# New hand-written orders for all five engines of an adaLN, attention and FFN kernel

## The reference, cut to what matters

```python
x = x + attn(moe(x, cond))       # 8 experts of width 64, top 2, and a shared one; banded linear attention; layer norm
x = x + ffn(attn2(x, mask, cond))  # 16 heads of 64, l2-normed q and k, position bias, softmax, layer norm
# attn2:
xn = ln(x, g_norm); q = xn @ Wq; k, v = split(xn @ Wkv)
sim = l2norm(q) * q_scale @ (l2norm(k) * k_scale).T * 8 + bias + causal mask
out = ln((softmax(sim) @ v) @ Wout, g_out)
# ffn: 128 -> 512 -> 512 -> 512 -> 128
h = silu(z @ w1 * s1) * (z @ w2 * s2)
h = gelu(h @ h1 * s); h = gelu(h @ h2 * s); return h @ w3 * s3
```

## Time and profile before

| | |
|---|---|
| three timed runs | 715.15, 715.75, 716.42 us, median 715.75 |
| profiled execution | 719.08 us, of which 717.1 us is the span from first to last instruction |
| mean granted TensorE clock | 0.983 of full |
| busy | TensorE 679.9, VectorE 547.5, ScalarE 528.1, GpSimd 359.6 us |
| fill, first pass | 0 to about 76.8, 76.8 to 136 us |
| a steady pass | 80.2 us |

### The profile page before, as it was taken

The page is one execution under the profiler, slowest core; times in us unless marked ns, Lnnn a source line. Parts: engine busy times, 40 slices in busy tenths (PEclk is TensorE's granted clock), DMA queues, the critical chain, the costliest instruction groups (busy, mean ns, idle before and its releaser), DMA issues.

```text
span 717.1 us, 20509 instructions
## 1 busy us (share of the span) xinstructions
PE 679.9 (95%) x7232; PEld 537.5 (75%) x7232; DVE 547.5 (76%) x1719; ACT 528.1 (74%) x1629; POOL 359.6 (50%) x410
## 2 busy tenths in 40 slices
...
GB/s 284 9 111 90 123 2 16 82 22 1 2 87 60 1 2 12 134 3 1 3 104 43 1 3 24 122 2 1 2 118 30 1 1 25 16 17 1 17 8 8
DMA packets 33587, 28.50 MB, mean 40 GB/s; under 512 B 4288, under 2 KB 29008, under 8 KB 33104
## 3 DMA queue, kind: packets, MB, share of 16 engines
...
...
## 4 chain that ended last, share of the span: by engine, by line
PE 57%; DVE 14%; ACT 9%; issue 7%; POOL 4%; DVEq 0%; ACTq 0%; POOLq 0%
PE ps_M L1314 30%; PE ps_z L1466 8%; DVE sb_sm L1187 5%; PE ps_S L1453 5%; PE ps_S L1438 4%; PE ps_M L1367 4%; PE ps_M L1498 3%; ACT sb_sm L830 3%; PE ps_S L1422 2%; PE ps_M L1397 2%; ACT sb_hT L795 2%; POOL sb_rq L697 1%; DVE sb_nmx L1194 1%; DVE sb_hAl L1024 1%; POOL sb_biasm L707 1%
## 5 line engine op out<-in xcount | busy, mean ns | idle before, releaser
L830 ACT ACTIVATE sb_sm<-sb_sm,sb_nmx 128x65 f32<-128x65 f32 (+3 forms) x512 | 178.1, 352 | 14.4 <-DVE sb_nmx L1194 14.1
L715 POOL TENSOR_TENSOR sb_sm<-sb_sm,sb_rden 128x128 f32<-128x128 f32 (+3 forms) x128 | 93.2, 738 | 126.4 <-DVE sb_rden L1198 126.1
L707 POOL TENSOR_TENSOR sb_biasm<-sb_bias,sb_maskn 128x128 f32<-128x128 f32 (+3 forms) x128 | 113.0, 894 | 49.6 <-DVE sb_maskn L1159 26.5
L1187 DVE SCALAR_TENSOR_TENSOR sb_sm<-ps_S,sb_rq,sb_biasm 128x65 f32<-128x65 f32 (+3 forms) x512 | 112.2, 292 | 24.0 <-PE ps_S L1438 19.5
L697 POOL TENSOR_TENSOR sb_rq<-sb_qss,sb_mhalf 128x16 f32<-128x16 f32 x32 | 93.6, 2949 | 28.8 <-DVE sb_qss L1169 28.8
L830 ACT ACTIVATION_READ_ACCUMULATOR sb_sm<-sb_sm,sb_nmx 128x1 f32 x512 | 97.1, 190 | 0.0
L1466 PE MATMUL ps_z<-sb_wout,sb_oT 128*128 128x128 f32 x512 | 69.1, 282 | 0.0
L1466 PEld LDWEIGHTS ps_z<-sb_wout,sb_oT 128*128 128x128 f32 x512 | 64.4, 193 | 4.3 <-ACT sb_oT L842 0.8
L842 ACT ACTIVATE sb_oT<-ps_S,sb_cols 128x256 f32<-128x256 f32 x128 | 52.9, 467 | 16.5 <-PE ps_S L1453 13.1
L1194 DVE TENSOR_REDUCE sb_nmx<-sb_sm 128x4 f32<-128x132 f32 (+3 forms) x128 | 59.3, 475 | 0.3
L767 ACT ACTIVATE sb_gs<-ps_M 128x512 f32<-128x512 f32 x39 | 23.2, 596 | 46.2 <-PE ps_M L1314 46.1
...
## 6 DMA issues: line engine op xcount, KB each, us to landing
...
sb_vrep<-values SPq DMA_DIRECT2D x16, 256.0 KB
sb_xg<-in_xT SPq DMA_DIRECT2D x8, 256.0 KB, 3.4
sb_xs<-in_x SPq DMA_DIRECT2D x8, 256.0 KB, 6.8
...
sb_hA<-in_h SPq DMA_DIRECT2D x2, 1024.0 KB, 7.2
out_y<-sb_res SPq DMA_DIRECT2D x7, 256.0 KB, 7.0
values<-sb_vs SPq DMA_DIRECT2D x16, 64.0 KB
```

Source lines behind the costliest of these rows:

```text
L707: pool.tensor_tensor(masked_bias(j % 4)[:, :, 1:wide], relative(bias0, i), maskn[:, j // 4, 0:wide - 1].unsqueeze(1).broadcast_to([128, 4, ...
L715: pool.tensor_tensor(p, p, stat(rden, g, j).unsqueeze(2).broadcast_to([128, 4, wide - 1]), ALU.mult)\
L830: ins = act.activation(p[:, t], p[:, t], ACT.Exp, bias=least[:, t:t + 1], accum_out=total[:, t:t + 1])
L1187: ins = dve.scalar_tensor_tensor(scored(g, j)[:, t], bank(g, "sim", n, odd)[:, first:first + wide], rq[:, col:col + 1], masked_bias(j % 4) ...
```

## The change

Of the 30 lists, 24 are written anew: all but the drain lists of TensorE, VectorE and GpSimd and the last three of SyncE. Each list holds exactly the items that it held before, in another order. Nothing else in the file is changed. [...] The lists that the prediction speaks of:

```diff
     "pe fill": """
-        lg.0 warm.0-2 pb.0-1 warm.3-6 rw.0 lg.1-2 exp.0-1 lg.3-4 exp.2 pb.2 lg.5-7 pb.3 exp.3-4 down.0 qkv.0
-        scores.0 mix.0 warm.7 fl.0-1 warm.8-10 fl.2 warm.11-13 xnT.0 warm.14 wr.0 warm.15-16 q.0 kv.0 q.1-4
-        qs.0-3 q.5-7 kT.0 warm.17 qs.4-7 warm.18-21
+        lg.0 pb.0 warm.0-4 rw.0 pb.1 lg.1-2 exp.0-1 lg.3 exp.2 lg.4 pb.2 lg.5 exp.3 lg.6-7 exp.4 pb.3 down.0
+        warm.5 qkv.0 scores.0 mix.0 warm.6 fl.0 warm.7-9 fl.1 warm.10-11 wr.0 warm.12-13 xnT.0 warm.14 fl.2
+        warm.15 kv.0 q.0-5 qs.0-3 q.6-7 warm.16 kT.0 warm.17 qs.4-7 warm.18-21
     "pe steady": """
-        sim.0 exp.0-3 sim.1 exp.4 down.0 zT.0 sim.2-3 qkv.0 l1.0 sim.4 l1.1 sim.5 l1.2-3 scores.0 l2.0-3 mix.0
-        PV.0 l3.0-2 sim.6-7 xnT.0 l3.3 kv.0 z.0 q.0 z.1 PV.1 l4.0 PV.2 q.1-2 z.2 q.3-4 qs.0-3 q.5-7 z.3 qs.4-7
-        kT.0 z.4 PV.3 z.5-7
+        sim.0 exp.0-1 sim.1 exp.2-4 down.0 zT.0 sim.2-3 qkv.0 l1.0 sim.4 l1.1 sim.5 l1.2-3 scores.0 l2.0-3 mix.0
+        PV.0 l3.0 sim.6-7 l3.1-2 xnT.0 l3.3 kv.0 q.0 z.0 PV.1 q.1 z.1 q.2 l4.0 z.2 PV.2 q.3-4 qs.0-3 q.5-7 z.3
+        qs.4-7 z.4 kT.0 PV.3 z.5-7
     "pe seventh": """
-        sim.0-1 exp.0 sim.2 exp.1-4 down.0 sim.3 zT.0 sim.4 qkv.0 scores.0 l1.0 sim.5 l1.1-3 mix.0 PV.0 l2.0
+        sim.0 exp.0-2 sim.1 exp.3 sim.2 exp.4 down.0 zT.0 sim.3 qkv.0 sim.4 l1.0 scores.0 l1.1-2 sim.5 l1.3
...
     "pe last": """
-        sim.0-2 l3p.2-3 sim.3-4 zT.0 l4p.0 l1.0 PV.0 l1.1 z.0 l1.2-3 z.1 l2.0 sim.5-6 l2.1-2 PV.1 l2.3 z.2 sim.7
+        sim.0-3 l3p.2-3 sim.4 zT.0 l4p.0 l1.0 PV.0 l1.1 z.0 l1.2-3 z.1 l2.0 sim.5-6 l2.1-2 PV.1 l2.3 z.2 l3.0
...
     "act start": """
-        xh.0 ph.4 rw.0 exp.0-2 ex.0 exp.3 ex.1 exp.4 ex.2-3 down.0 ex.4 qkv.0 ex.5-6 ph.5 ex.7 PV.0 ex.8 PV.1
+        xh.0 ph.4 rw.0 exp.0-2 ex.0 exp.3 ph.5 ex.1 exp.4 ex.2-3 down.0 qkv.0 ex.4-7 PV.0 ex.8 PV.1 ex.9 ln2.0
...
     "dve fill": """
-        cg.0 pb.0 rt.0 x0.0 pb.1 rt.1-4 rw.0 pl.0 wl.0 pb.2 exp.0 pb.3 exp.1 nk.0 exp.2 rt.5 exp.3 pl.1 rt.6
-        exp.4 rt.7 down.0 xl.0 rt.8 maskn.0 qkv.0 scores.0 mix.0 pl.2 ln1.0 rt.9 xnT.0 pl.3 nk.1 q.0 kv.0 q.1-4
-        vs.0 q.5-7 ssq.0 ssc.0
+        cg.0 pb.0 rt.0 pb.1 rt.1-4 rw.0 wl.0 x0.0 pl.0 exp.0 pb.2 exp.1 pb.3 xl.0 pl.1 nk.0 exp.2-3 rt.5 exp.4
+        rt.6-7 down.0 rt.8 qkv.0 scores.0 mix.0 ln1.0 rt.9 pl.2-3 xnT.0 kv.0 q.0-3 maskn.0 nk.1 q.4-7 vs.0 ssq.0
+        ssc.0
     "dve start": """
-        rw.0 xl.0 pl.4 exp.0 sim.0 exp.1 max.0 exp.2 inv.0 max.1 exp.3 sim.1 inv.1 max.2 exp.4 max.3 sim.2 tp.0
+        rw.0 xl.0 pl.4 exp.0 sim.0 exp.1 max.0 exp.2 inv.0 max.1 exp.3 sim.1 inv.1 max.2 exp.4 max.3 sim.2
...
     "pool start": """
-        bias.4-5 pn.0 bias.6 pn.1 xb.0 bias.7-8 pn.2-4 bias.9 pn.5-6 bias.10 ln1.0 pn.7 bias.11-12 ln2.0
+        bias.4-5 pn.0-1 bias.6-7 pn.2 bias.8-9 pn.3 bias.10 pn.4 bias.11 ln1.0 bias.12 xb.0 bias.13 pn.5-6 ln2.0
...
     "sp fill": """
-        hw.0 lx.0 ls.0 vst.0 wr.0 lm.0 vb.0-1
+        lx.0 ls.0 hw.0 vst.0 vb.0 wr.0 lm.0 vb.1
     "sp start": """
-        hw.1 lx.0 ls.0 wb.0 vst.0 vb.0 lm.0 vb.1
+        lx.0 hw.1 wb.0 vst.0 vb.0 lm.0 ls.0 vb.1
     "sp steady": """
-        vst.0 lx.0 wb.0 vb.0 ls.0 l4.0 vb.1 lm.0
+        vst.0 vb.0 wb.0 ls.0 l4.0 lm.0 lx.0 vb.1
```

More of the change, by code:

```diff
@@ L64 @@
+        warm.15 kv.0 q.0-5 qs.0-3 q.6-7 warm.16 kT.0 warm.17 qs.4-7 warm.18-21
     """,
     "pe start": """
-        rw.0 exp.0 sim.0-1 exp.1-3 sim.2 exp.4 down.0 sim.3-4 qkv.0 scores.0 mix.0 PV.0 sim.5-6 z.0 xnT.0 PV.1
-        q.0 z.1 sim.7 z.2 kv.0 q.1 PV.2 z.3 q.2-3 z.4 PV.3 q.4 qs.0-3 q.5-7 z.5 qs.4-7 kT.0 z.6-7
+        rw.0 exp.0 sim.0-1 exp.1-3 sim.2 exp.4 down.0 sim.3 qkv.0 scores.0 mix.0 sim.4 PV.0 sim.5-6 z.0 xnT.0
+        z.1 PV.1 q.0 sim.7 z.2 kv.0 PV.2 q.1 z.3 q.2 z.4 q.3 z.5 PV.3 q.4 qs.0-3 q.5-7 qs.4-7 kT.0 z.6-7
@@ L86 @@
     "act fill": """
-        wh.0 xh.0 rx.0 ph.0 pb.0-1 rw.0 exp.0 pb.2 exp.1 pb.3 exp.2 ph.1 exp.3 rx.1 pb.4 exp.4 ph.2 down.0 qkv.0
-        fl.0 ph.3 ln2.0 fl.1-2 xnT.0 wr.0 q.0-3 kd.0 q.4-7 kT.0
+        xh.0 rx.0 pb.0 wh.0 pb.1 ph.0 rw.0 exp.0-2 ph.1 pb.2 exp.3 pb.3 ph.2 exp.4 rx.1 pb.4 down.0 qkv.0 fl.0
+        ph.3 ln2.0 fl.1 wr.0 xnT.0 fl.2 q.0-3 kd.0 q.4-7 kT.0
     """,
     "act start": """
-        xh.0 ph.4 rw.0 exp.0-2 ex.0 exp.3 ex.1 exp.4 ex.2-3 down.0 ex.4 qkv.0 ex.5-6 ph.5 ex.7 PV.0 ex.8 PV.1
@@ L102 @@
-        q.5-7 ex.12-15 PV.4-5 l3.0 kd.0 l3.1 PV.6-7 kT.0
+        xh.0 exp.0-1 ex.0 exp.2 ex.1 exp.3-4 ex.2-3 down.0 zT.0 ex.4-5 qkv.0 ex.6 l1.0 h1.0 l1.1-2 h1.1-2 l1.3
+        ex.7 h1.3 PV.0-1 ex.8-10 l2.0 ln2.0 h2.0 xnT.0 l2.1-2 h2.1 PV.2 h2.2 q.0-1 PV.3 q.2-3 l2.3 ex.11 q.4-6
+        h2.3 q.7 ex.12-15 PV.4-5 kd.0 l3.0-1 PV.6-7 kT.0
     """,
     "act last": """
-        ex.0-3 l3p.2-3 ex.4 zT.0 ex.5-6 l1.0 PV.0 l1.1 h1.0-1 l1.2 PV.1 l1.3 h1.2-3 ex.7-10 l2.0 h2.0 PV.2 l2.1
-        h2.1 PV.3 l2.2-3 h2.2-3 ex.11-13 l3.0-3 zTd.0 ex.14-15 l1d.0 PV.4 l1d.1 h1d.0 PV.5 h1d.1 l1d.2 h1d.2
@@ L123 @@
+        tp.0-1 inv.2-3 down.0 sim.3 max.4 tp.2 max.5 tp.3 qkv.0 inv.4 scores.0 max.6 tp.4 inv.5 max.7 mix.0
+        sim.4 inv.6-7 max.8 ln1.0 tp.5 max.9 sim.5 inv.8 tp.6-7 max.10 sim.6 max.11 inv.9 maskn.0 xnT.0 tp.8
+        max.12 inv.10 tp.9 inv.11 tp.10 max.13 tp.11 sim.7 inv.12 max.14 q.0 inv.13 max.15 kv.0 tp.12 inv.14
+        tp.13 inv.15 tp.14-15 q.1-2 pl.5 q.3-7 ssq.0 ssc.0 vs.0
     """,
     "dve steady": """
-        xl.0 ln3.0 sim.0 exp.0-1 max.0-1 exp.2-3 sim.1 exp.4 max.2 zT.0 max.3 inv.0-2 down.0 zl.0 sim.2 max.4
@@ L126 @@
[L126 to L129, removed]
+        xl.0 ln3.0 sim.0 exp.0 max.0 exp.1 max.1 exp.2-3 sim.1 exp.4 max.2 zT.0 max.3 inv.0-1 down.0 zl.0 sim.2
```

68 lines of the change are left out of this document (35 added, 33 removed).

## The result

| | us |
|---|---|
| before, on the same chip | median 716.09 (715.15 to 718.72, 4 runs) |
| after | median 725.45 (723.06 to 730.28, 4 runs) |
| ratio | 1.0133, 95% interval 1.0073 to 1.0193 |
| predicted | 719.6, range 712.5 to 727 |

The sign and the place are those of the forecast, the size is not: +9.4 us measured, +3.9 forecast.

The account below looks back on a forecast made before the run. TensorE, busy 95% of its 717.1 us span, was taken as the bound. Fill and first pass +4.0, steady +1.0, seventh -1.8, last pass +0.7 sum to +3.9: median 715.75 becomes 719.6, range 712.5 to 727.

Parts of the forecast that it names:

- First pass, the term that decides: First pass: early ph.5 makes ScalarE wait 4.4 us for h2, exp.4 +3.7; fill and first pass together +4.0.
- the prediction's own sign: First pass, profile after: ScalarE idle 3 to 5 us at about 84 to 89, ended by the DMA into sb_hA.
- The clock behind the wait: First pass: qkv's matmuls at the low clock after longer idle time, only in the upper bound of +6.5.
- Fill, -1.8: Fill: low-clock stretch gone (1.4), first expert about 1.0 earlier, wr ahead of xnT 0.6 late; bounds -3.5 and +1.0.
- The row of "lg" items: Fill: three "lg" items in a row from 28.74, then low clock 31.0 to 34.4; spreading them might save 1.4 us.
- Its difference is laid on 715.75: Whole kernel: the sum is made against the profiled 719.08 us and its difference applied to the timed median.
- Steady, +1.0: Five steady passes: TensorE's new order costs +0.2 a pass; lx moved later costs nothing.
- Rival 2: Steady passes: lx lands late, exp.0 up to 2.2 us late in each of five; 724.6, at worst 730; chance 0.14.
- Seventh, -1.8: Seventh pass: 0.7 wait and small ones removed, a second VectorE wait covered, shorter switches; bounds -2.5 and +1.0.
- The 0.7 wait: Seventh pass: TensorE's longest wait, for VectorE, removed by exp.0-1 standing ahead of sim.1.
- Last pass, +0.7: Last pass: sim.3 waits for VectorE +1.0, 0.5 back at l4p, zT in the drain +0.2; bounds -0.5 and +1.5.
- Rival 1: First pass: h2 lands in time, its load taking 4.8 instead of 9.5 us; 713 to 714.9, say 713.7; chance 0.27.

Follow-up runs that it names:

- e1: After, with only ScalarE's copy of raw h2 (ph.5) moved back to its old place between ex.6 and ex.7; 717.9 us, ratio 1.0014.
- e4: After, with the load of h2 issued straight behind the store of the values, ahead of both spreads, ph.5 still early; 716.4 us, ratio 0.9987.
- e2: Before, with only ScalarE's copy of raw h2 (ph.5) moved to its new place right behind exp.3; 719.92 us, ratio 1.0047.
- r1: After, with only vs.0 moved back in VectorE's fill list, from behind q.7 to behind q.3; 720.73 us, ratio 1.0051.
- r2: After, with the load of h2 issued behind the first of the two spreads, ahead of wr, lm, the second spread and lx; 720.63 us, ratio 1.0047.
- g1: After, with h2 loaded early as in e4, SyncE's old steady list (lx second) and last-pass sim.3 behind l3p.2-3; 714.06 us, ratio 0.9962.
- f0: After, unchanged, timed again; 726.59 us, ratio 1.0131 to before.
- f1: After, with twelve more warm items (24 unused 128x128 matmuls) on TensorE between exp.4 and down in the first pass; 722.11 us, ratio 1.0087.
- e3: Before, with all five new fill lists and no other change; 716.37 us, ratio 0.9997.
- r3: As g1, with the old fill lists except that the load of h2 stands behind the store of the values; 714.84 us, ratio 0.998.

## Why the prediction was right in sign and short in size

- **First pass, the term that decides: the mechanism right, the size half.** Shown by undoing it (e1, e4) and by doing it alone (e2). The step that failed is the wait (the prediction's own sign was 3 to 5 us idle on ScalarE), 4.4 us forecast, 8.20, 7.28 and 7.13 in the three traces with after's lists. The landing itself was forecast at 88.7 and came at 88.74, but that is a coincidence of two errors. Counted from the end of vs.0 (69.80) it took 18.9 us, not the forecast 15.7: 4.6 instead of 3.5 until the first spread, 2.9 instead of 2.7 to the load, 11.5 instead of 9.5 to land. And the fill ended 2.9 us earlier than I had it, so ScalarE stood ready at 80.6, not 84.3. A wait is a difference of two times, and I carried the absolute times of an execution with a slow fill through the sum. From the start of the first expert to the landing of h2 it is 11.4 us in before, 11.6 in e2, 16.7, 15.8 and 15.6 with after's lists, 12.7 in r1, 11.0 in r2 and 7.0 in e4 and g1: that difference belongs to the lists and hardly moves with the clock. In the two first traces fill and first pass together went from 136.0 to 141.6, +5.6 against the +4.0 forecast, which looks close only because the fill of before was slow in its trace.
- **The clock behind the wait: priced only as a bound**, "qkv at the low clock" at the far end of the range, and at nothing in the sum. In after's trace it came, and cost 0.9 us at qkv; in f0's the low stretch ended where qkv starts, and it cost nothing there. Filling 5.5 us of the 6.6 us of idle time (f1) took the stretch away and made the median 4 us lower, but how much of that is this stretch stays open: f1's first pass is as long as f0's.
- **Fill, -1.8: refuted.** The early low stretch did go, in the profiled execution, and the fill came out 4.7 shorter; e3 (0.9997) and the table show that the stretches lie otherwise from execution to execution. The row of "lg" items does not bring the stretch by itself, as I had it: e2 and r3 have the old order and no low stretch at 31 us, while e3, e4, f0 and r2 have the new one and a low stretch between 18.9 and 26.7. What goes with that one is a late landing of the 2 MB load (see e3). "Its difference is laid on 715.75" suffers from it too: the trace of before, from which I took the times, had 13.6 us of low clock in its fill, that of e2 with the same fill lists 6.8.
- **Steady, +1.0: net nothing in the first trace (401.7 both), from two parts that cancel.** The new orders gain 0.8 (400.8 to 401.1 with SyncE's old list), where I had forecast a loss of 0.2 a pass. lx late costs 0.1 to 2.1 us in all, 1.1 in the mean of the six traces; in after's own trace it is one pass of 81.1, whose xh waits 0.58 us for x. Rival 2 is real at a fifth of its price: in no pass was the whole 8.0 us of mask paid.
- **Seventh, -1.8: refuted.** 73.8 and 73.9. The 0.7 wait shrank to 0.5, and 1.1 for ScalarE at l1 and 0.8 for VectorE at xnT stand beside it: 2.5 us of waits before, 2.6 after.
- **Last pass, +0.7: 1.6 and 1.8 measured, by another way.** The wait of 1.09 at sim.3 came as forecast (+1.0), but all but 0.2 of it is given back at l4p, and the other new lists there gain 1.0. What the longer traces have in common is the low stretch that comes with two waits in a row, 1.3 to 1.6 us when it is 3.4 long and about 2.8 when it is 6.9.
- **Rival 1** (h2 in time) did not happen; e4 shows what it would have given had it. I had 713.7 for it, and it is 716.4, as the seventh's gain in it doesn't exist. (My sentence that by the page "the sum would be the second rival's" means this one, the first.) By the Trainium skill's price, "DMA: Bandwidth & Descriptors", section "Anatomy of one DMA", an estimate of 4.4 us for 1 MB, the load would have been in time. The runs agree with that within 0.8 with no spread ahead (4.8 to 5.2) and not with one or two (8.9 to 11.5).
- "I am wrong if the first steady sim starts before 137 us": 141.56.

The sum of what was found, against 716.0: first pass +10.3 and +6.9 in the two traces of after, last pass +1.6 and +1.8: 727.9 and 724.7; measured 725.5 and 726.6 in the median. Two traces of one kernel differ by 3.4 us in the first pass, so the sum is no closer than that.
